# Causal layer of a four-layer kernel: operand loads of batches 1 to 3 moved to ScalarE's queue in column pieces, scores and maxima alternated, block sums of first tiles put later

## The chip, the cores and the metric

One core of a Trainium2 chip runs the whole program in one launch. The metric is device time in microseconds (us), the median of three runs; lower is better.

## The reference, cut to what matters

x has shape (4, 512, 128): four batches of 512 tokens. Four layers are added to it in turn: a selective-scan layer, an attention layer with a mixture of experts, the **causal layer** that this change touches, and the attention and expert layer once more. The causal layer is:

```
h = layernorm(x);  q, k, v = split(h @ Wqkv.T + bqkv)      # 16 heads of 8
q, k = rotary(q), rotary(k)                                # first 2 of the 8 dims
probs = softmax(q @ k.T / sqrt(8) + causal_mask)
L = eye - strict_lower(probs);  rhs = diag(probs) * v
A = solve_triangular(L, rhs, lower=True)
x = x + concat_heads(A) @ Wd.T + bd
```

So row i of A depends on all rows before it: the layer is a forward substitution over the 512 positions of each batch, with the softmax's normalisation carried beside it.

## The kernel before, in words

The causal layer is `delta_phase`. A batch has four tiles of 128 positions (`TPB` = 4), 16 tiles in all, numbered n = 0 to 15, with t = n % 4 the place of the tile in its batch. All engines run one loop over n from -6 to 15, each turn of it divided into 14 hooks h = 0 to 13. Every engine executes its instructions in the order written, so the hooks are the schedule; there is no planner. Turn n solves tile n: `from_earlier` (h = 0, the part that comes from the batch's earlier tiles), `turn_right_side` (h = 1), `inverse` (h = 2) and seven `hop`s (h = 3, 5, 7, 9, 10, 11, 12), each followed on VectorE by `turned_hop`. At h = 12 ScalarE copies the result (`solved`, L2439) and at the start of the next turn it copies the turned result into `a_all` (`turned`, L2443), which the next tile's `from_earlier` on TensorE (L2880) reads.

Around this chain, `beside` prepares later tiles. For tile m = n + 3 TensorE computes the scores (`score`, L2789 and L2798) and ScalarE their exponentials (L2389, L2394); for tile m = n + 3 (t = 0) or n + 4 it computes the scores once more without shift, for the row maxima (`for_maximum`, L2768 and the mask L2771), which VectorE reduces (L2546). The functions `scores_in` and `maxima_in` say which groups fall to which hook; within a hook TensorE issues all scores, then all maxima. Scores leave through two PSUM banks, maxima through three. VectorE adds up the exponentials of the tile's own block (`block_sums`, L2582), then `own_sum`, `spread_sums`, and from these `inverted_sums`, with which GpSimd inverts 16x16 blocks (`inverse_block`); SyncE carries them through DRAM (`inverses`, L2296 and L2303) into `xT`, which `multiplied` (L2832, h = 9 to 12 of the turn before) reads.

The operands `q_op` and `k_op` hold one batch: for each head, 72 rows of three-part bf16 queries or keys by 512 positions, in one buffer each. In turn n = 4b - 4 (n = 0, 4, 8) SyncE stores the split queries and keys of batch b into `q_scr` and `k_scr` (`store_parts`, L2257), waits for these stores, and then runs `operands(b)`: for each half of the heads, once the last tile's scores of that half are done, one DMA of queries (L2271, 576 KB) and three of keys (L2274, 192 KB each). TensorE waits for a half at the first maximum of tile 4b that uses it (groups 0 and 2, at h = 3 and h = 5 of turn 4b - 3). Behind `operands`, SyncE's next work is `inverses(n + 2)` of the turn that follows. For batch 0 another way is used: three pieces by columns (positions), the queries of the first two on SyncE's queue (L2264), the keys and the last queries on ScalarE's (L2367, L2371).

The block sums of a tile with t = 0 are taken at h = 0 and 1 of turn m - 2; its own sum at h = 1, spread at h = 3, inverted at h = 4.

The functions as they stand before, with the line numbers of the profile:

Of the kernel before, what the change touches and what calls it, by code (L numbers as in the profile page):

```python
# [6 lines left out]

# [1914 lines left out]
def delta_phase(core, nc):  # L1922
# [4 lines left out]
    with ExitStack() as ctx:  # L1927
        def sb(name, shape, dt=F32):
# [48 lines left out]
                 "first_in0 first_in1 first_in2 op_in0 op_in1 bias_out m_split diff_out eii_out vn_out m_stored m_in_even m_in_odd sums_out z_out z_spread e_stored e_in "  # L1977
# [56 lines left out]
        def in_program(n):  # L2034
            return 0 <= n < TILES_N
# [28 lines left out]
        def block_sums_in(n, h):  # L2064

            first, second = n + 2, n + 3
            if second == 0:
                return [(0, 2 * (h - 11)), (0, 2 * (h - 11) + 1)] if h in (11, 12) else []
            if first == 0:
                return [(1, 2 * (h - 8)), (1, 2 * (h - 8) + 1)] if h in (8, 9) else []  # L2070
            if in_program(first) and first % TPB == 0 and h < 2:
                return [(first, 2 * h), (first, 2 * h + 1)]
# [28 lines left out]
        def spread_at(m):  # L2101
            return {0: (-3, 13), 1: (-2, 13)}.get(m, (m - 2, 3))

        def own_sum_at(m):
            return {0: (-3, 13), 1: (-2, 12)}.get(m, (m - 2, 0 if m % TPB else 1))

        def inverted_at(m):
            return {0: (-2, 1), 1: (-1, 1)}.get(m, (m - 2, 4))
# [86 lines left out]
        with nc.Block() as block:  # L2195
# [56 lines left out]
            def _(sp):  # L2252
# [14 lines left out]
                def operands(b):  # L2267
                    for half in range(2):
                        sp.wait_ge(s["act_ps"], in_act("score", b * TPB - 1, DIAG_GROUPS + (half + 1) * NH // 2 - 1))
                        heads = heads_of(half)  # L2270
                        sp.dma_start(q_op[0:QK_ROWS, heads, :], query_rows(q_scr[b, :, :, heads, :])).then_inc(  # L2271
                            s[f"op_in{half}"], 16)
                        for i in range(PARTS):
                            sp.dma_start(k_op[rows_of_part(i), heads, :], key_rows(k_scr[b, :, :, heads, :])).then_inc(  # L2274
                                s[f"op_in{half}"], 16)

# [31 lines left out]
                for n in range(-LEAD, TILES_N):  # L2308
# [8 lines left out]
                    if in_program(n + 4) and n % TPB == 0:  # L2317
                        store_parts((n + 4) // TPB)
                        if n + 4 == 0:
                            first_queries()  # L2320
                        else:
                            operands((n + 4) // TPB)
# [8 lines left out]
            def _(act):  # L2331
# [30 lines left out]
                def first_keys():  # L2362
                    act.wait_ge(s["parts_stored"], 16 * 2 * PARTS)
                    act.wait_ge(s["pad_in"], 32)
                    for piece, cols in enumerate(FIRST_COLS):
# [3 lines left out]
                        if piece == 2:  # L2369
                            for i in range(PARTS):  # L2370
                                act.dma_start(q_op[i:QK_ROWS:PARTS, :, cols], query_columns(q_scr[0, :, :, :, cols])).then_inc(  # L2371
                                    s[f"first_in{piece}"], 16)

# [75 lines left out]
                for n in range(-LEAD, TILES_N):  # L2449
# [6 lines left out]
                    for h in range(HOOKS):  # L2456
# [258 lines left out]
            def _(pe):  # L2715
# [40 lines left out]
                def for_maximum(n, g):  # L2756
# [6 lines left out]
                    if n >= TPB and t == 0 and g * heads in (0, NH // 2):  # L2763
                        pe.wait_ge(s[f"op_in{2 * g * heads // NH}"], 16 * (1 + PARTS) * b)
# [72 lines left out]
                def beside(n, h):  # L2837
# [13 lines left out]
                    for i in scores_in(n, h):  # L2851
                        score(n + 3, i)
                    for m, hd in maxima_in(n, h):
                        for_maximum(m, hd)
# [183 lines left out]
```

## Time and profile before

| | |
|---|---|
| median of 3 runs | 1435.49 us (1435.31 to 1438.86) |
| profiled execution, its own time | 1435.48 us |
| its span, first to last instruction | 1433.6 us |
| TensorE busy | 1141.3 us (80%) |
| VectorE busy | 987.3 us (69%) |
| ScalarE busy | 684.4 us (48%) |
| GpSimd busy | 630.1 us (44%) |
| mean granted TensorE clock | 0.887 of full |
| causal layer | from about 628 to 1108 us of the span |

Times in the rows are microseconds from the start of the span. "Idle before" in brackets is how long the engine stood before that instruction, and what released it. Busy shares say little here: TensorE is busy most of the time, and what a change in the causal layer is worth is read from the places where TensorE stands still.

### The profile page before, as it was taken

To read this page: it belongs to the slowest core of one execution; us is meant where nothing else is said; L and a number is where in the kernel's file an instruction comes from. 1 tells how busy PE (TensorE), PEld (TensorE's weight loads), DVE (VectorE), ACT (ScalarE), POOL (GpSimd) and SP (SyncE) were. 2 spreads that over 40 slices of the span, in tenths; PEclk is the share of its full clock that TensorE was granted. 3 is DMA by queue.
4 is the path that set the end of the run, shared out by engine and by line. 5 is a ranking of instruction groups with operands and counts; after the bars stand their busy time and mean duration, and the time that the engine had idled before them with its cause. 6 is when DMAs were issued, how large, how long until landed. Compare 5 with 4: busy or idle time off the path is not lost. (4 is left out here: it accounts for less than half of the span.)

```text
span 1433.6 us, 32921 instructions
## 1 busy us (share of the span) xinstructions
PE 1141.3 (80%) x12875; PEld 621.9 (43%) x12906; DVE 987.3 (69%) x2114; ACT 684.4 (48%) x1412; POOL 630.1 (44%) x838
## 2 busy tenths in 40 slices
PE   6746767769999998833767988878986799999975
PEld 2212222323333335822555665656665233333375
DVE  5699999978888875544745746646521798888453
ACT  3843334414776776621442442343341277676744
POOL 2268979954235212521632533533441533251153
PEclk9869979978999999865898978989987599999988
DMA  5388934132141402244242141141120232240222
GB/s 154 134 287 317 330 118 179 37 90 57 37 105 55 105 3 91 66 99 89 32 85 46 28 107 26 29 105 26 28 44 11 70 91 58 68 119 22 86 56 87
DMA packets 133279, 128.22 MB, mean 89 GB/s; under 512 B 87543, under 2 KB 119095, under 8 KB 127738
## 3 DMA queue, kind: packets, MB, share of 16 engines
q1 hardware_dynamic: 125072, 118.24, 29.8%
q0 software_dynamic: 2496, 5.13, 1.1%
q10 hardware_dynamic: 5558, 2.76, 0.9%
q8 instruction: 102, 1.67, 0.5%
q14 instruction: 51, 0.42, 0.1%
HBM read 105.42 MB, written 38.49 MB: 100 GB/s over the span
## 5 line engine op out<-in xcount | busy, mean ns | idle before, releaser
L1402 DVE TENSOR_REDUCE f_row_min<-f_ps 128x1 f32<-128x512 f32 x512 | 327.7, 682 | 63.8 <-PE f_ps L1722 63.1
L1284 ACT ACTIVATE f_e<-f_ps 128x512 f32<-128x512 f32 x512 | 278.7, 598 | 124.3 <-PE f_ps L1741 123.4
L1722 PE MATMUL f_ps<-f_operands 72*128 72x512 bf16 x512 | 205.0, 411 | 20.5 <-DMA f_operands<-k_scr 15.3
L1741 PE MATMUL f_ps<-f_operands 75*128 75x512 bf16 x512 | 190.0, 381 | 2.6 <-ACT f_e L1284 2.6
L789 PE MATMUL m_ps<-m_shared,sb_ident 128*128 128x512 f32 x256 | 134.7, 674 | 60.6 <-DVE m_shared L629 60.6
L362 POOL TENSOR_TENSOR m_drive<-m_du,m_ring 128x1024 f32<-128x1024 f32 x64 | 149.5, 2349 | 57.1 <-DVE m_ps L621 37.5
L2546 DVE TENSOR_REDUCE d_row_min<-d_ps 128x1 f32<-128x384 f32 (+3 forms) x176 | 105.2, 635 | 60.6 <-PE d_ps L2771 59.1
L494 ACT ACTIVATE m_ps<-m_delta,m_A 128x511 f32<-128x511 f32 x128 | 83.0, 681 | 132.7 <-DVE m_ps L621 109.0
L1752 PE MATMUL f_ps<-f_e,f_v_op 128*32 128x512 f32 x1024 | 137.2, 607 | 2.4 <-ACT f_e L1284 1.4
L1722 PEld LDWEIGHTS f_ps<-f_operands 72*128 72x128 bf16 x512 | 51.3, 101 | 162.9 <-DVE f_row_min L1402 111.8
L789 PEld LDWEIGHTS m_ps<-m_shared,sb_ident 128*128 128x128 f32 x256 | 52.2, 214 | 145.4 <-DVE m_shared L629 89.5
L621 DVE TENSOR_TENSOR_SCAN m_ps<-m_ps,m_drive 128x1024 f32<-128x1024 f32 x44 | 101.1, 2297 | 4.9
L2768 PE MATMUL d_ps<-d_k_op,d_q_op 96*128 96x128 bf16 (+3 forms) x256 | 68.2, 346 | 29.4 <-DMA d_k_op<-k_scr 17.0
L2696 DVE STREAM_TRANSPOSE d_a_hop<-d_ps 128x32 f32<-128x32 f32 x112 | 23.8, 213 | 83.6 <-PE d_ps L2921 71.5
L2921 PE MATMUL d_ps<-d_mT,d_a_hop 16*32 16x16 f32 (+3 forms) x3584 | 67.6, 209 | 8.4 <-DVE d_a_hop L2696 7.5
L2225 POOL TENSOR_TENSOR d_xT_blk<-d_xT_blk,d_prod 128x14 f32<-128x14 f32 (+6 forms) x224 | 64.7, 289 | 17.6
L1172 POOL DMA_INDIRECT y_scr<-f_operands x46 | 53.5, 1164 | 40.5 <-DVE f_operands L1612 38.5
L1741 PEld LDWEIGHTS f_ps<-f_operands 75*128 75x128 bf16 x512 | 49.6, 99 | 49.1 <-ACT f_e L1284 20.3
L2214 POOL TENSOR_TENSOR d_xT_blk<-d_e_blk,d_zi_blk 128x256 f32<-128x256 f32 x16 | 14.3, 893 | 126.1 <-DVE d_zi_blk L2611 124.0
L2220 POOL TENSOR_TENSOR d_prod<-d_xT_blk 128x14 f32<-128x14 f32 (+6 forms) x224 | 60.6, 271 | 17.6
L2832 PE MATMUL d_ps<-d_xT,d_e_nat 128*32 128x128 f32 (+3 forms) x2048 | 58.6, 263 | 12.1 <-DMA d_xT<-x_scr 5.4
L1146 POOL DMA_INDIRECT f_rows_scr<-f_h2n,f_place_u x32 | 31.7, 990 | 82.6 <-DVE f_place_u L1520 74.9
(297 smaller groups left out, 2162.7 us busy)
## 6 DMA issues: line engine op xcount, KB each, us to landing
m_ring<-bc_scr SPq DMA_DIRECT2D x32, 1024.0 KB, 5.2
f_rows_scr<-blank SPq DMA_DIRECT2D x2, 8707.5 KB, 31.4
f_wall<-f_wall SPq DMA_DIRECT2D x16, 578.0 KB, 5.0
f_operands<-q_scr SPq DMA_DIRECT2D x32, 288.0 KB
f_operands<-k_scr SPq DMA_DIRECT2D x96, 96.0 KB
d_q_op<-q_scr SPq DMA_DIRECT2D x6, 576.0 KB
d_k_op<-k_scr SPq DMA_DIRECT2D x18, 192.0 KB
f_operands<-f_rows_scr SPq DMA_DIRECT2D x46, 64.5 KB, 1.9
```

Source lines behind the costliest of these rows:

```text
L362: nc.gpsimd.tensor_tensor(drive[:, step % AHEAD, :].rearrange("p (a s) -> p a s", a=HALVES), du[:, :, tokens(b)], b_row(step).unsqueeze(1) ...
L494: last = nc.scalar.activation(ps[:, at + 1:at + S], delta[:, k, b * S + 1:(b + 1) * S], ACT.Exp, scale=A[:, k, n:n + 1])
L621: nc.vector.tensor_tensor_scan(h, bank(DECAY + HALVES * (step % 2), HALVES), drive[:, step % AHEAD, :], 0.0, ALU.mult, ALU.add).then_inc(s ...
L789: last = nc.tensor.matmul(bank(Y + k), core.ident[:, :], hC[:, k * S:(k + 1) * S], start=False, stop=last_of_batch)
L1284: nc.scalar.activation(e_sb[:, n % 3, hh, :], ps[:, SCORE[(b * UNITS + u) % SCORE_BANKS], :], ACT.Exp, scale=SCALE).then_inc(s["e_out"], 1)
L1402: nc.vector.tensor_reduce(row_min[:, b % 2, u // TPB, u % TPB:u % TPB + 1], ps[:, MAXQ[(b * UNITS + u) % MAX_BANKS], :], AX.X, ALU.max, ne ...
L1722: nc.tensor.matmul(ps[:, MAXQ[n % MAX_BANKS], :], q_op(b, QK)[:, hd, t * P:(t + 1) * P], k_op(b, QK)[:, hd, :], start=True, stop=True).the ...
L1741: nc.tensor.matmul(ps[:, SCORE[n % SCORE_BANKS], :], k_op(b, QKS)[:, hd, t * P:(t + 1) * P], q_op(b, QKS)[:, hd, :], start=True, stop=True ...
L1752: last = nc.tensor.matmul(ps[hh * HEAD_COLS:(hh + 1) * HEAD_COLS, O_BANK, :], v_of(b, t, g * GROUP + hh), e_sb[:, n % 3, hh, :], start=(t ...
L2546: nc.vector.tensor_reduce(row_min[:, n % 2, g * heads:(g + 1) * heads], dve_bank("maximum", n, g)[:, 0:heads * cols].rearrange("p (h c) -> ...
L2768: nc.tensor.matmul(bank[:, hh * cols:(hh + 1) * cols], q_op[0:SHIFT_AT, hd, rows_of(t)], k_op[0:SHIFT_AT, hd, 0:cols], start=(hh == 0), st ...
L2921: last = nc.tensor.matmul(ps[q * SPAN:(q + 1) * SPAN, STEP[n % 2], r * SPAN + cols.start:r * SPAN + cols.stop], a_hop[own, g * SPAN:(g + 1 ...
```

## The change

For the batches 1, 2 and 3, `operands` is gone from SyncE. ScalarE issues the loads instead, twelve DMAs for each batch in four steps by columns: queries of positions 0 to 383 after h = 12 of turn 4b - 4, keys of positions 0 to 127 after its h = 13, and after h = 1 of turn 4b - 3 the keys of positions 128 to 511 and the queries of 384 to 511. Each step is three DMAs. The first six count on one semaphore, for which the first maximum of tile 4b waits; the last six on another, for which the first maximum of tile 4b + 1 waits (h = 6 of the same turn). In each hook TensorE now takes one score and one maximum in turn. The block sums of tiles with t = 0 (but the first) move from h = 0 and 1 to h = 2 and 3, their own sum from h = 1 to 3, spread from 3 to 4 and inversion from 4 to 5.

```
@@ -4,6 +4,7 @@
 
 
 from contextlib import ExitStack, contextmanager
+from itertools import zip_longest
 
 import numpy as np
 
@@ -1974,7 +1975,7 @@
         aT = sb("aT", [P, 2, P])
 
         names = ("set zero_set pad_in ln_stats ln_mv ln_var ln_rstd ln_done swapped rot1 rot2 rot3 prod_out split_q split_k parts_stored "
-                 "first_in0 first_in1 first_in2 op_in0 op_in1 bias_out m_split diff_out eii_out vn_out m_stored m_in_even m_in_odd sums_out z_out z_spread e_stored e_in "
+                 "first_in0 first_in1 first_in2 first_cols_in other_cols_in bias_out m_split diff_out eii_out vn_out m_stored m_in_even m_in_odd sums_out z_out z_spread e_stored e_in "
                  "blk_step x_stored x_in g_ps gT_sb gn_ps gn_sb at_ps hop_in at_sb an_ps an_sb "
                  "act_ps act_out dve_ps dve_out").split()
         s = {n: core.sem("d_" + n) for n in names}
@@ -2068,8 +2069,8 @@
                 return [(0, 2 * (h - 11)), (0, 2 * (h - 11) + 1)] if h in (11, 12) else []
             if first == 0:
                 return [(1, 2 * (h - 8)), (1, 2 * (h - 8) + 1)] if h in (8, 9) else []
-            if in_program(first) and first % TPB == 0 and h < 2:
-                return [(first, 2 * h), (first, 2 * h + 1)]
+            if in_program(first) and first % TPB == 0 and h in (2, 3):
+                return [(first, 2 * (h - 2)), (first, 2 * (h - 2) + 1)]
             if in_program(second) and second % TPB and h in (8, 9, 12, 13):
                 return [(second, (8, 9, 12, 13).index(h))]
             return []
@@ -2099,13 +2100,13 @@
             return (-2, 12) if m == 1 else (m - 2, 2)
 
         def spread_at(m):
-            return {0: (-3, 13), 1: (-2, 13)}.get(m, (m - 2, 3))
+            return {0: (-3, 13), 1: (-2, 13)}.get(m, (m - 2, 3 if m % TPB else 4))
 
         def own_sum_at(m):
-            return {0: (-3, 13), 1: (-2, 12)}.get(m, (m - 2, 0 if m % TPB else 1))
+            return {0: (-3, 13), 1: (-2, 12)}.get(m, (m - 2, 0 if m % TPB else 3))
 
         def inverted_at(m):
-            return {0: (-2, 1), 1: (-1, 1)}.get(m, (m - 2, 4))
+            return {0: (-2, 1), 1: (-1, 1)}.get(m, (m - 2, 4 if m % TPB else 5))
 
         def batch_at(place, n, h):
             return next((b for b in range(B) if place(b) == (n, h)), None)
@@ -2264,16 +2265,6 @@
                             sp.dma_start(q_op[i:QK_ROWS:PARTS, :, cols], query_columns(q_scr[0, :, :, :, cols])).then_inc(
                                 s[f"first_in{piece}"], 16)
 
-                def operands(b):
-                    for half in range(2):
-                        sp.wait_ge(s["act_ps"], in_act("score", b * TPB - 1, DIAG_GROUPS + (half + 1) * NH // 2 - 1))
-                        heads = heads_of(half)
-                        sp.dma_start(q_op[0:QK_ROWS, heads, :], query_rows(q_scr[b, :, :, heads, :])).then_inc(
-                            s[f"op_in{half}"], 16)
-                        for i in range(PARTS):
-                            sp.dma_start(k_op[rows_of_part(i), heads, :], key_rows(k_scr[b, :, :, heads, :])).then_inc(
-                                s[f"op_in{half}"], 16)
-
                 def shifts(n):
                     t = n % TPB
                     sp.wait_ge(s["act_out"], in_act("shifts", n))
@@ -2318,8 +2309,6 @@
                         store_parts((n + 4) // TPB)
                         if n + 4 == 0:
                             first_queries()
-                        else:
-                            operands((n + 4) // TPB)
                     if in_program(n + 4) and (n + 4) % TPB != 0:
                         shifts(n + 4)
                     if in_program(n + 3) and (n + 3) % TPB == 0:
@@ -2370,6 +2359,17 @@
                             for i in range(PARTS):
                                 act.dma_start(q_op[i:QK_ROWS:PARTS, :, cols], query_columns(q_scr[0, :, :, :, cols])).then_inc(
                                     s[f"first_in{piece}"], 16)
+
+                def queries(b, cols, after, done):
+                    act.wait_ge(s["act_ps"], all_scores(after))
+                    act.wait_ge(s["parts_stored"], 16 * 2 * PARTS * (b + 1))
+                    for i in range(PARTS):
+                        act.dma_start(q_op[i:QK_ROWS:PARTS, :, cols], query_columns(q_scr[b, :, :, :, cols])).then_inc(done, 16)
+
+                def keys(b, cols, after, done):
+                    act.wait_ge(s["act_ps"], all_scores(after))
+                    for i in range(PARTS):
+                        act.dma_start(k_op[rows_of_part(i), :, cols], key_rows(k_scr[b, :, :, :, cols])).then_inc(done, 16)
 
                 def own_exponential(n):
                     act.wait_ge(s["diff_out"], n + 1)
@@ -2459,6 +2459,16 @@
                             from_earlier(n)
                         if n >= 0 and HOP_AFTER.get(h) == HOPS:
                             solved(n)
+                        b = starts_in(n, 4)
+                        if b is not None and b >= 1:
+                            if h == 12:
+                                queries(b, slice(0, S - P), TPB * b - 2, s["first_cols_in"])
+                            if h == 13:
+                                keys(b, slice(0, P), TPB * b - 1, s["first_cols_in"])
+                        b = starts_in(n, 3)
+                        if b is not None and b >= 1 and h == 1:
+                            keys(b, slice(P, S), TPB * b - 1, s["other_cols_in"])
+                            queries(b, slice(S - P, S), TPB * b - 1, s["other_cols_in"])
 
             @block.vector
             def _(dve):
@@ -2760,8 +2770,10 @@
                         pe.wait_ge(s["pad_in"], 32)
                     if n < len(FIRST_COLS) and g == 0:
                         pe.wait_ge(s[f"first_in{n}"], 16 * 2 * PARTS)
-                    if n >= TPB and t == 0 and g * heads in (0, NH // 2):
-                        pe.wait_ge(s[f"op_in{2 * g * heads // NH}"], 16 * (1 + PARTS) * b)
+                    if n >= TPB and t == 0 and g == 0:
+                        pe.wait_ge(s["first_cols_in"], 16 * 2 * PARTS * b)
+                    if n >= TPB and t == 1 and g == 0:
+                        pe.wait_ge(s["other_cols_in"], 16 * 2 * PARTS * b)
                     bank = dve_free("maximum", n, g)
                     for hh in range(heads):
                         hd = g * heads + hh
@@ -2848,10 +2860,11 @@
                     m = maxima_done(n, h - 1)
                     if m is not None:
                         turn_shifts(m)
-                    for i in scores_in(n, h):
-                        score(n + 3, i)
-                    for m, hd in maxima_in(n, h):
-                        for_maximum(m, hd)
+                    for i, maximum in zip_longest(scores_in(n, h), maxima_in(n, h)):
+                        if i is not None:
+                            score(n + 3, i)
+                        if maximum is not None:
+                            for_maximum(*maximum)
                     if in_program(n + 1) and h in MT_HOOKS:
                         multiplied(n + 1, MT_HOOKS.index(h))
                     m = later_tile_at(sums_at, n, h)
```

## Rows read from the trace of the kernel before

**Rows 1.** Turns 1 and 3 by stretch: length, busy (x) of PE, PEld, DVE, ACT, POOL, PEclk, DMA share, GB/s.

```profile
740.40:775.50 35.10, 23.27 (x577) 16.87 (x582) 12.31 (x39) 5.34 (x16) 9.58 (x31) 0.81 0.43 78
...
797.80:824.40 26.60, 24.82 (x614) 17.74 (x616) 17.51 (x42) 11.27 (x25) 13.75 (x41) 0.98 0.17 30
```

**Rows 2.** Waits of PE, 640 to 1110: us in total, times, longest.

```profile
PE d_ps L2768 <- DMA d_k_op<-k_scr: 17.0, 5, 5.1
```

**Rows 3.** Timeline of PE, batch 1: start, us, instructions, idle before.

```profile
744.09 0.37 PE L2880 MATMUL d_ps<-d_e_off,d_a_all 128*32 128x128 f32 x3
...
752.69 0.61 PE L2768 MATMUL d_ps<-d_k_op,d_q_op 96*128 96x128 bf16 x4 [5.13 <-DMA d_k_op<-k_scr]
...
759.69 0.61 PE L2768 MATMUL d_ps<-d_k_op,d_q_op 96*128 96x128 bf16 x4 [4.02 <-DMA d_k_op<-k_scr]
...
762.95 0.60 PE L2768 MATMUL d_ps<-d_k_op,d_q_op 96*128 96x256 bf16 x2
```

**Rows 4.** Timeline of PE, batch 2.

```profile
854.42 1.06 PE L2880 MATMUL d_ps<-d_e_off,d_a_all 128*32 128x128 f32 x32
...
857.66 0.40 PE L2768 MATMUL d_ps<-d_k_op,d_q_op 96*128 96x128 bf16 x4
...
864.67 0.61 PE L2768 MATMUL d_ps<-d_k_op,d_q_op 96*128 96x256 bf16 x2
```

**Rows 5.** Timeline of PE, batch 3.

```profile
956.86 0.82 PE L2880 MATMUL d_ps<-d_e_off,d_a_all 128*32 128x128 f32 x18
...
962.47 0.40 PE L2768 MATMUL d_ps<-d_k_op,d_q_op 96*128 96x128 bf16 x4 [1.18 <-DMA d_k_op<-k_scr]
...
968.95 0.61 PE L2768 MATMUL d_ps<-d_k_op,d_q_op 96*128 96x128 bf16 x4 [4.72 <-DMA d_k_op<-k_scr]
...
972.20 0.60 PE L2768 MATMUL d_ps<-d_k_op,d_q_op 96*128 96x256 bf16 x2
```

**Rows 6.** Timeline of SP's queue: first operand load of batches 1, 2, 3.

```profile
740.04 0.86 SPq L2271 DMA_DIRECT2D d_q_op<-q_scr  x1
...
845.58 0.88 SPq L2271 DMA_DIRECT2D d_q_op<-q_scr  x1
...
951.91 0.85 SPq L2271 DMA_DIRECT2D d_q_op<-q_scr  x1
```

**Rows 7.** Timeline of ACT at the end of turns 0, 4, 8.

```profile
741.06 0.27 ACT L2443 COPY d_a_all<-d_ps 128x128 f32<-128x128 f32 x1 [0.42 <-PE d_ps L2931]
...
850.97 0.27 ACT L2439 COPY d_aT<-d_ps 128x128 f32<-128x128 f32 x1
...
953.40 0.27 ACT L2439 COPY d_aT<-d_ps 128x128 f32<-128x128 f32 x1
```

**Rows 8.** Timeline of ACT's DMA issues for batch 0.

```profile
651.19 7.59 ACTq L2367 DMA_DIRECT2D d_k_op<-k_scr  x9
...
658.81 4.31 ACTq L2371 DMA_DIRECT2D d_q_op<-q_scr  x3
```

**Rows 9.** Stretches with operand loads (columns as in rows 1): batches 1, 2, 0.

```profile
740.00:760.00 20.00, 9.69 (x245) 7.31 (x239) 2.97 (x11) 1.44 (x5) 3.86 (x13) 0.79 0.66 127
845.00:861.00 16.00, 13.03 (x403) 10.86 (x395) 4.37 (x14) 3.17 (x9) 3.69 (x10) 0.82 0.66 160
...
652.00:668.40 16.40, 7.69 (x39) 4.62 (x39) 7.66 (x17) 0.47 (x2) 1.94 (x2) 0.57 0.87 144
```

**Rows 10.** DMA packets, 740 to 760, then 652 to 668.5.

```profile
DMA packets 531, 2.54 MB, mean 127 GB/s; under 512 B 112, under 2 KB 240, under 8 KB 240
...
DMA packets 7156, 2.37 MB, mean 144 GB/s; under 512 B 4883, under 2 KB 7155, under 8 KB 7155
```

**Rows 11.** Timeline of DVE, turn 2.

```profile
779.90 1.27 DVE L2582 TENSOR_REDUCE d_z_col<-d_e_nat 128x4 f32<-128x512 f32 x2
```

**Rows 12.** Waits of PE, turn 6.

```profile
PE d_ps L2832 <- DMA d_xT<-x_scr: 1.6, 1, 1.6
PE d_ps L2908 <- DVE d_g_pad L2687: 1.3, 1, 1.3
```

More of the change, by code:

```diff
@@ L6 @@
 from contextlib import ExitStack, contextmanager
+from itertools import zip_longest
 import numpy as np
@@ L2070, in block_sums_in @@
                 return [(1, 2 * (h - 8)), (1, 2 * (h - 8) + 1)] if h in (8, 9) else []
-            if in_program(first) and first % TPB == 0 and h < 2:
-                return [(first, 2 * h), (first, 2 * h + 1)]
+            if in_program(first) and first % TPB == 0 and h in (2, 3):
+                return [(first, 2 * (h - 2)), (first, 2 * (h - 2) + 1)]
             if in_program(second) and second % TPB and h in (8, 9, 12, 13):
@@ L2265, in first_queries @@
                                 s[f"first_in{piece}"], 16)
[L2267 to L2275, printed above, removed]
                 def shifts(n):
@@ L2320, in _ @@
                             first_queries()
-                        else:
-                            operands((n + 4) // TPB)
                     if in_program(n + 4) and (n + 4) % TPB != 0:
@@ L2372, in first_keys, with queries, keys @@
                                     s[f"first_in{piece}"], 16)
+                def queries(b, cols, after, done):
+                    act.wait_ge(s["act_ps"], all_scores(after))
+                    act.wait_ge(s["parts_stored"], 16 * 2 * PARTS * (b + 1))
+                    for i in range(PARTS):
+                        act.dma_start(q_op[i:QK_ROWS:PARTS, :, cols], query_columns(q_scr[b, :, :, :, cols])).then_inc(done, 16)
+                def keys(b, cols, after, done):
+                    act.wait_ge(s["act_ps"], all_scores(after))
+                    for i in range(PARTS):
+                        act.dma_start(k_op[rows_of_part(i), :, cols], key_rows(k_scr[b, :, :, :, cols])).then_inc(done, 16)
                 def own_exponential(n):
@@ L2461, in _ @@
                             solved(n)
+                        b = starts_in(n, 4)
+                        if b is not None and b >= 1:
+                            if h == 12:
+                                queries(b, slice(0, S - P), TPB * b - 2, s["first_cols_in"])
+                            if h == 13:
+                                keys(b, slice(0, P), TPB * b - 1, s["first_cols_in"])
+                        b = starts_in(n, 3)
+                        if b is not None and b >= 1 and h == 1:
+                            keys(b, slice(P, S), TPB * b - 1, s["other_cols_in"])
+                            queries(b, slice(S - P, S), TPB * b - 1, s["other_cols_in"])
             @block.vector
@@ L2850, in beside @@
                         turn_shifts(m)
[L2851 to L2854, printed above, removed]
+                    for i, maximum in zip_longest(scores_in(n, h), maxima_in(n, h)):
+                        if i is not None:
+                            score(n + 3, i)
+                        if maximum is not None:
+                            for_maximum(*maximum)
                     if in_program(n + 1) and h in MT_HOOKS:
```

14 lines of the change are left out of this document (8 added, 6 removed).

## The prediction

> **What bounds the kernel now.** I read the page first, for the share of each engine, and then went to the causal layer alone, since only that is touched. TensorE executes in order and carries the chain of the substitution, so a turn lasts as long as TensorE needs, its standstills included. The stretches by turn show this: turn 3, with scores and maxima side by side, has TensorE busy 24.8 of 26.6 us, while turn 1, the first after an operand load, takes 35.1 us with 23.3 busy [rows 1]. The reader is to see that the time to be had is in the turns 1, 5 and 9, not in turn 3. TensorE's waits over the whole layer name the cause: 17.0 us in five waits for the keys [rows 2].
>
> The timelines of these turns show what the waits hang on. In batch 1 TensorE stands 5.1 us before the first maximum of tile 4 (free from 747.56) and 4.0 us before the third group, and reaches the first maximum of tile 5 at 762.95 [rows 3]. In batch 2 the first maximum comes without a wait at 857.66, the tile after at 864.67 [rows 4]. In batch 3 the waits are 1.2 and 4.7, the first maximum of the next tile is at 972.20 [rows 5]. That leaves 17.0 - 5.1 - 4.0 - 1.2 - 4.7 = 2.0 us for batch 2's second half; the work after that wait is the same as from 759.69 to 762.95, 3.3 us, so that half was in by 864.67 - 3.26 = 861.4. The queue of SyncE began the loads at 740.04, 845.58 and 951.91 [rows 6]. From first issue to the last operand the loads thus take 19.7, 15.8 and 17.0 us, mean 17.5. The second half is the one that decides, and tile 4b + 1 starts 3.3 us after it has landed.
>
> **The operand loads.** The same bytes move (2304 KB), so the question is when they start, how long they last and who must wait for the last of them.
>
> Start. ScalarE issues the first six DMAs after its copy `solved` of h = 12. This copy ends at 741.06 - 0.42 = 740.64 in batch 1, and at 851.24 and 953.67 in batches 2 and 3 [rows 7]. Against SyncE's starts [rows 6] the loads begin 0.6, 5.7 and 1.8 us later. The wait for the parts' stores costs ScalarE nothing, since SyncE had passed the same wait before those moments; behind it stand `turned` and `from_earlier`, which the chain needs.
>
> Issue. Nine of ScalarE's issues for batch 0 took 7.59 us, 0.84 each; the last three, queued behind all the others, 4.31, that is 1.44 each [rows 8]. These are the bounds: 5.0 to 8.6 us for six. With an emptier queue I take the lower, 5.0. They lie in front of `turned`, so `a_all` comes at 745.9 instead of 741.3. TensorE's `from_earlier` started only at 744.09 because other sums came first [rows 3], so the chain moves by 745.98 - 744.09 = 1.9 us, not by 5. In the same way by 2.2 in batch 2 (854.42, [rows 4]) and 2.1 in batch 3 (956.86, [rows 5]). TensorE is then ready for tile 4b at 749.5, 859.9 and 963.4 (962.47 - 1.18 + 2.1). The last six issues follow the copy for h = 0, end by about 753, and ScalarE's next needed work (h = 7) comes later; they cost nothing unless an issue costs 1.44.
>
> Duration. Batch 0 is loaded by columns already, in two thirds of its DMAs by runs of 256 bytes. It moved 144 GB/s against 127 and 160 in the loads by heads [rows 9], with 7156 packets against 531 [rows 10]; from 651.19 to 668.4 it took 17.2 us. In the new form a quarter of the bytes go in 256-byte runs, in batch 0 half; I take 0.7 us off: 16.5. New beside the load is `inverses`, no longer queued behind it: 128 KB for `xT` (L2303) now move at the same time, 128/2304 of 17.5 us = 1.0 us. Sum 17.5 us from the end of `solved` to the last operand; from below 13.5 (the first 1.2 us and 2.36 MB at 200 GB/s, above any whole load of rows 9), from above 20.7 (the 19.7 of batch 1 and the 1.0).
>
> At this place a rule speaks against the change. The Trainium skill, page "DMA: Bandwidth & Descriptors", section Specifications, wants at least 512 bytes in a transfer for line rate, and its section "Rules for kernel authors" says that spreading DMAs over SP and ACT brings no bandwidth, for they end on the same 16 engines. On the first the trace doesn't agree at this size: 144 GB/s in small runs beside 127 in large ones. On the second no stretch contradicts it, and my sum gives the queue no bandwidth. By the first the duration would be at the upper end, which is a rival below.
>
> Who waits. Tile 4b needs the first half (queries to 383 and keys to 127, 1.18 MB), which by half the duration is in at about 750, 860.7 and 963.4: hardly later than TensorE is ready. TensorE then works 6.2 us to tile 5 in batch 1 (3.0 from 752.69 to the second wait, 3.3 behind it), about 5.1 in the others: ready at 755.9, 865.8 and 968.5. The rest lands at 740.64 + 17.5 = 758.1, at 868.7 and at 971.2, later in all three, so the new wait, at the first maximum of tile 4b + 1, ends last. Against 762.95, 864.67 and 972.20: -4.8, +4.0 and -1.0, sum **-1.8 us**. The gain is that 3.3 us of work now lie before the last landing and not behind it; in batch 2 the later start eats it. Bounds by the durations: -9.7 (data in by 754.1, 864.7 and 967.2, TensorE ready later; deltas -7.1, +1.1, -3.7) and +7.8 (three times 3.2, less 1.8).
>
> **The clock.** In the stretch of batch 1's load the granted clock was 0.79 and in turn 1 0.81, while turn 3 had 0.98 [rows 1, 9]: it falls between the waits. The new waits are shorter in batch 1 (2.2 us instead of 9.1) and of 2.9 and 2.7 us in the others. I take **-1.0 us**; bounds 0 and -4.
>
> **Scores and maxima in turn.** The order changes only where a hook has several scores: turns -1, 3, 7 and 11. In turns 2, 6, 10 a hook has one score, and in turns 0, 1, 4, 5 scores and maxima do not meet. In turn 3 TensorE is idle 26.60 - 24.82 = 1.8 us in all [rows 1]; that is the upper bound, and a reordering that starves the exponentials could cost as much. I take -0.2 for each of four, **-0.8 us**, bounds -3 and +2.
>
> **Block sums later.** In turn 2 VectorE does two pairs of block sums, 1.27 us each [rows 11], before it adds the right side; in turn 6 TensorE waits 1.3 us for that sum [rows 12]. The edit removes this wait, but puts the 1.27 us in front of `turned_hop` of h = 2 and h = 3, where VectorE is nearly full. In turn 6 TensorE also waits 1.6 us for `xT` [rows 12], which hangs on SyncE's order and would take back what is gained before it. I take **0**; bounds for three batches -3.9 and +3.9. Spread and inversion one hook later delay GpSimd's block inversion by about 2 us, which is hidden: its result is wanted a turn later.
>
> **Sum.** -1.8 - 1.0 - 0.8 + 0 = -3.6. Against the profiled execution's own 1435.48 us (span 1433.6 and 1.9 around it; the median of the runs, 1435.49, is the same) that is 1431.9, so **1432 us**.
>
> **Rivals.** (1) The load is quicker by columns. If its rate is 200 GB/s, the new waits vanish, -9.7 us; with a clock that stays up (-3) and the order of scores (-0.8) the time is 1422. For it: one load by heads reached 160 GB/s with few rows in flight, and the runs are now longer than batch 0's. Against it: no load of the trace came near. (2) The load is as slow as batch 1's or the small runs hurt: 20.7 us from `solved`, +7.8 instead of -1.8, no help from the clock, 1435.5 + 7.8 - 0.8 = 1442. This is also what the page's rule on 512 bytes would do. For it the 127 GB/s of batch 1, against it the 144 of batch 0 [rows 9]. (3) The other side by ScalarE: its issues cost 1.44 us each. Twelve take 17.3 us, 1.9 lie between the sixth and the seventh, and the last needs some 2 us to land: 21.2 us from `solved`, 3.7 more than forecast in each batch, +11.1 - 1.8 - 0.8 = +8.5, **1444**. It decides as soon as an issue costs over (17.5 - 3.9)/12 = 1.13 us, because then the issue and not the transfer ends last. For it the last three of batch 0, against it the nine before [rows 8].
>
> **Chances.** Forecast 0.40, rival 1 0.30, rival 2 0.16, rival 3 0.14. The likeliest case alone spans 1427 to 1438. What a measurement here can tell from no change is about 0.3%, 4.3 us: below 1431.2 faster, above 1439.8 slower. Of the forecast's 0.40, 0.12 lie below, 0.26 within, 0.02 above; rival 1 is all faster; rivals 2 and 3 give 0.25 slower and 0.05 within. Faster 0.42, same 0.31, slower 0.27. The range takes in both sides, 1420 to 1444.
>
> **What would show it.** Right: the waits for keys at tiles 4, 8, 12 gone or under 1 us, a new wait at the first maximum of tiles 5, 9 and 13, longest in batch 2; six ScalarE issues of about 0.84 us between `solved` and `turned`; `from_earlier` some 2 us later; turn 5 longer than 28 us, turn 1 shorter than 35.1; turn 3 within 1 us of 26.6. Wrong: issues above 1.1 us, or a load that ends under 15 or over 19 us after `solved`. A VectorE transpose at h = 3 of turn 2 that makes TensorE wait over 1 us would show the block sums' price.

## The result and the profile after

The changed kernel takes 1443.09 us in the median of 20 runs (1436.07 to 1448.37); the kernel before, run beside it, 1434.3 (20 runs). The ratio is 1.0053, 95% interval 1.0034 to 1.0073: **0.5% slower, some 7.6 us**. Forecast was 1432.0, a small gain. The time lies inside the predicted range, near its upper end; the sign is wrong.

The profiled execution has a span of 1444.6 us (1433.6 before), a mean granted TensorE clock of 0.876 (0.887) and an own time of 1446.39. A turn below reaches from one copy `solved` to the next. The turns are added up by their place in the batch, because the first turn of a batch holds the wait for the operands and the second the later block sums:

| us, sum of turns | 1, 5, 9 | 2, 6, 10 | 3, 7, 11 | 4, 8, 12 | 13 to 15 |
|---|---|---|---|---|---|
| before | 93.8 | 68.9 | 79.3 | 76.9 | 48.1 |
| after | 97.8 | 77.4 | 77.4 | 75.5 | 47.4 |

The turns explain +8.5 of the +11.0 us of span. The rest is -0.6 ahead of turn 1 and +3.1 in the attention layer behind, which the change does not touch. The turns 1, 5 and 9, which hold the loads, cost 4.0 us here, **and the turns 2, 6 and 10, for which the forecast put 0, cost 8.5**.

The turns 1, 2 and 11 of after by stretch (columns as in [rows 1]):

```profile
740.10:773.60 33.50, 26.05 (x585) 18.89 (x585) 12.76 (x39) 5.28 (x15) 9.62 (x31) 0.75 0.46 78
773.60:799.40 25.80, 21.43 (x532) 15.64 (x530) 18.53 (x56) 8.64 (x19) 9.39 (x31) 0.87 0.21 34
...
1018.20:1042.90 24.70, 22.72 (x595) 15.84 (x589) 15.76 (x41) 11.37 (x25) 11.18 (x34) 1.00 0.16 26
```

and the turns 2 and 11 of before:

```profile
775.50:797.80 22.30, 18.81 (x530) 14.09 (x532) 18.15 (x56) 8.73 (x19) 7.80 (x24) 1.00 0.22 33
...
1006.90:1033.40 26.50, 24.10 (x602) 16.82 (x592) 15.92 (x41) 11.30 (x26) 12.09 (x38) 0.96 0.16 27
```

Turn 2 has the same 530 matmuls, but they are busy for 21.4 us instead of 18.8, at a clock of 0.87 instead of 1.00; TensorE stands 4.4 us instead of 3.5. Over the turns 2, 6 and 10 it is busy 64.2 us instead of 56.3 and idle 13.2 instead of 12.6. So nearly all of the 8.5 us is the same work done more slowly. A lost turn has two parts, idle time and slower work behind it, and the waits below show only the first.

TensorE's waits from 640 to 1120 us, after (us in total, times, longest); [rows 2] is their counterpart:

```profile
PE d_ps L2780 <- DMA d_q_op<-q_scr: 15.9, 5, 10.6
PE d_ps L2833 <- DVE d_z_spread L2614: 11.0, 4, 2.8
PE d_ps L2780 <- DMA d_k_op<-k_scr: 8.8, 3, 4.1
PE d_ps L2893 <- ACT d_a_all L2443: 5.0, 3, 1.8
PE d_ps L2921 <- DVE d_g_pad L2697: 2.3, 6, 0.5
```

Of the first row, all but 4.7 belongs to batch 0, which did not change. The wait for keys is halved (17.0 to 8.8), but three others stand beside it: 4.7 for the last queries, 5.0 for `a_all`, and `z_spread` at 11.0 (8.3 of it in turns 2, 6 and 10), which before was 4.9 in all. The place is in the timeline of TensorE, turn 2:

```profile
784.63 0.61 PE L2833 MATMUL d_ps<-sb_in_block,d_z_spread 128*128 128x16 f32 x2 [2.78 <-DVE d_z_spread L2614]
...
785.46 0.63 PE L2801 MATMUL d_ps<-d_k_op,d_q_op 128*128 128x128 bf16 x4
```

The score matmul of the last line took 0.39 us at 781.02, before the stand, and 0.63 after it. The stretches around it show the clock fall from full speed (2.4 GHz) to half (1.2 GHz) and come back:

```profile
778.00:781.70 3.70, 3.41 (x84) 2.37 (x82) 3.70 (x9) 1.23 (x3) 0.00 (x0) 1.00 0.16 20
784.50:788.00 3.50, 3.37 (x40) 2.52 (x43) 1.72 (x9) 0.60 (x1) 0.27 (x1) 0.50 0.35 33
788.00:792.00 4.00, 4.00 (x71) 2.76 (x64) 2.42 (x7) 1.46 (x3) 3.37 (x10) 0.65 0.31 35
792.00:799.40 7.40, 6.16 (x267) 5.01 (x265) 6.33 (x20) 3.66 (x10) 5.75 (x22) 1.00 0.11 26
```

The wait itself is short and takes the place of others; the 7.5 us behind it run at 0.50 and 0.65. What VectorE did ahead of it:

```profile
778.88 1.27 DVE L2592 TENSOR_REDUCE d_z_col<-d_e_nat 128x4 f32<-128x512 f32 x2
...
780.20 0.98 DVE L2556 TENSOR_REDUCE d_row_min<-d_ps 128x1 f32<-128x384 f32 x2
781.10 1.27 DVE L2592 TENSOR_REDUCE d_z_col<-d_e_nat 128x4 f32<-128x512 f32 x2
782.40 0.18 DVE L2597 TENSOR_TENSOR d_z_col<-d_z_col,d_eii 128x16 f32<-128x16 f32 x1
782.49 0.87 DVE L2488 BATCH_NORM_STATS2 d_stats<-x 128x6 f32<-128x128 f32 x4
...
783.40 0.98 DVE L2556 TENSOR_REDUCE d_row_min<-d_ps 128x1 f32<-128x384 f32 x2
784.29 0.28 DVE L2614 TENSOR_TENSOR d_z_spread<-d_z_col,sb_blocks 128x128 f32<-128x128 f32 x1
```

VectorE has hardly a gap from 778.88 to 784.57 (the lines left out are two transposes of 0.20 us). The spread comes last in that queue, and TensorE's `sums_by_block` (L2833, called with the inversion, h = 5 now instead of 4) waits for it. TensorE has other work, but it stands behind this one in program order.

The loads, in ScalarE's timeline of batch 1 ([rows 7] has the copies of before):

```profile
739.73 0.27 ACT L2439 COPY d_aT<-d_ps 128x128 f32<-128x128 f32 x1
739.79 2.59 ACTq L2367 DMA_DIRECT2D d_q_op<-q_scr  x3
742.42 2.36 ACTq L2372 DMA_DIRECT2D d_k_op<-k_scr  x3
744.83 0.27 ACT L2443 COPY d_a_all<-d_ps 128x128 f32<-128x128 f32 x1 [4.83 <-issue]
...
746.30 3.46 ACTq L2372 DMA_DIRECT2D d_k_op<-k_scr  x3
749.85 5.03 ACTq L2367 DMA_DIRECT2D d_q_op<-q_scr  x3
```

and where TensorE meets them, batches 1, 2 and 3 (two waits each; before: [rows 3 to 5]):

```profile
752.53 0.61 PE L2780 MATMUL d_ps<-d_k_op,d_q_op 96*128 96x128 bf16 x4 [4.05 <-DMA d_k_op<-k_scr]
759.01 0.61 PE L2780 MATMUL d_ps<-d_k_op,d_q_op 96*128 96x256 bf16 x2 [0.37 <-DMA d_q_op<-q_scr]
863.11 0.61 PE L2780 MATMUL d_ps<-d_k_op,d_q_op 96*128 96x128 bf16 x4 [2.01 <-DMA d_k_op<-k_scr]
870.46 0.39 PE L2780 MATMUL d_ps<-d_k_op,d_q_op 96*128 96x256 bf16 x2 [1.23 <-DMA d_q_op<-q_scr]
970.05 0.61 PE L2780 MATMUL d_ps<-d_k_op,d_q_op 96*128 96x128 bf16 x4 [2.70 <-DMA d_k_op<-k_scr]
978.79 0.61 PE L2780 MATMUL d_ps<-d_k_op,d_q_op 96*128 96x256 bf16 x2 [3.06 <-DMA d_q_op<-q_scr]
```

### The profile page after: what moved, and what is told of

The parts are those of the page before. It is cut to its first block and busy times, and to the rows that moved or that the text cites. A ratio compares the mean times of both kernels' runs of the same rounds, so it can differ in the third digit from the quotient of the medians.

```text
span 1444.6 us, 32970 instructions
## 1 busy us (share of the span) xinstructions
PE 1159.1 (80%) x12906; PEld 632.5 (44%) x12906; DVE 988.9 (68%) x2114; ACT 685.3 (47%) x1412; POOL 630.2 (44%) x838
## 5 line engine op out<-in xcount | busy, mean ns | idle before, releaser
L2780 PE MATMUL d_ps<-d_k_op,d_q_op 96*128 96x128 bf16 (+3 forms) x256 | 75.8, 371 | 25.0 <-DMA d_q_op<-q_scr 15.9
L2934 PE MATMUL d_ps<-d_mT,d_a_hop 16*32 16x16 f32 (+3 forms) x3584 | 70.6, 214 | 11.8 <-DVE d_a_hop L2706 6.9
L2226 POOL TENSOR_TENSOR d_xT_blk<-d_xT_blk,d_prod 128x14 f32<-128x14 f32 (+6 forms) x224 | 64.7, 289 | 17.5
L2221 POOL TENSOR_TENSOR d_prod<-d_xT_blk 128x14 f32<-128x14 f32 (+6 forms) x224 | 60.8, 272 | 17.6
L2389 ACT ACTIVATE d_e_nat<-d_ps 128x512 f32<-128x512 f32 x64 | 37.3, 597 | 62.9 <-PE d_ps L2801 61.9
```

The source lines that it names most:

```text
L2780: nc.tensor.matmul(bank[:, hh * cols:(hh + 1) * cols], q_op[0:SHIFT_AT, hd, rows_of(t)], k_op[0:SHIFT_AT, hd, 0:cols], start=(hh == 0), st ...
L2934: last = nc.tensor.matmul(ps[q * SPAN:(q + 1) * SPAN, STEP[n % 2], r * SPAN + cols.start:r * SPAN + cols.stop], a_hop[own, g * SPAN:(g + 1 ...
```

## The experiments

Each ratio is against the kernel before, run beside it in five rounds. Turn sums come from one profile each; for 1, 5, 9 they scatter (85.5 to 99.6 in four kernels with identical loads: before, e2, e3 and e11), so there the ratios decide.

| | ratio, 95% interval | 1, 5, 9 | 2, 6, 10 | 3, 7, 11 |
|---|---|---|---|---|
| after | 1.0053, 1.0034 to 1.0073 | 97.8 | 77.4 | 77.4 |
| e1 | 1.0017, 0.9993 to 1.0042 | 100.2 | 67.0 | 78.0 |
| e2 | 1.0041, 1.0017 to 1.0065 | 85.5 | 75.2 | 79.2 |
| e3 | 0.9981, 0.9956 to 1.0006 | 99.6 | 71.4 | 76.0 |
| e4 | 1.0044, 1.0017 to 1.0071 | 97.1 | 68.9 | 79.6 |
| e5 | 0.9968, 0.9938 to 0.9999 | 92.4 | 67.4 | 80.0 |
| e6 | 1.0035, 1.0005 to 1.0066 | 97.6 | 72.9 | 75.2 |
| e7 | **0.9960, 0.9933 to 0.9986** | 88.9 | 68.1 | 77.1 |
| e8 | 1.0041, 1.0011 to 1.0071 | 100.6 | 67.0 | 80.4 |
| e9 | 1.0002, 0.9974 to 1.0030 | 90.5 | 68.3 | 80.4 |
| e10 | 1.0036, 1.0009 to 1.0064 | 94.0 | 67.8 | 79.6 |
| e11 | 1.0025, 0.9998 to 1.0053 | 86.2 | 69.3 | 81.0 |
| e12 | 1.0018, 0.9996 to 1.0041 | 90.8 | 77.4 | 77.0 |

**e1, all but the block sums.** The four places of tiles with t = 0 back in the changed kernel (the pair h in (2, 3) again h < 2, own sum 1, spread 3, inversion 4).

```
-            if in_program(first) and first % TPB == 0 and h in (2, 3):
+            if in_program(first) and first % TPB == 0 and h < 2:
...
-            return {0: (-3, 13), 1: (-2, 13)}.get(m, (m - 2, 3 if m % TPB else 4))
+            return {0: (-3, 13), 1: (-2, 13)}.get(m, (m - 2, 3))
...
```

> The changed kernel with only the block sums back at their old hooks (loads on ScalarE and the alternation stay). Theory A: turns 2, 6, 10 fall from 77.4 to about 69, the ratio to before is 0.999 to 1.003. Theory B: turns 2, 6, 10 stay above 74, ratio 1.004 or more.

The turns 2, 6 and 10 fell from 77.4 to 67.0: their length hangs on the block sums. What is left of the change (loads and order) could not be told from no change.

**e2, the block sums alone** in the kernel before: the mirror image of e1.

> The kernel before with only the block sums of tiles 4, 8 and 12 put two hooks later (own sum at h = 3, spread at 4, inversion at 5). Theory A (the block sums' place is the main loss: in turn 2 TensorE waits at sums_by_block for the spread): turns 2, 6, 10 together 6 to 9 us longer than before's 68.9, a wait of TensorE for L2604 of 2 to 3 us in each, other turns unchanged; ratio about 1.005. Theory B (the loss comes from the loads, and the long turn 2 is their echo: tile 4's scores finish late): turns 2, 6, 10 within 1.5 us of 68.9, ratio 1.000.

1439.7 against 1433.82 us, +5.9, turns 2, 6 and 10 at 75.2, with clocks of 0.93, 0.87 and 0.93. The two waits they trade, 700 to 1120 us:

```profile
PE d_ps L2821 <- DVE d_z_spread L2604: 8.3, 3, 2.8
...
PE d_ps L2908 <- DVE d_g_pad L2687: 2.3, 6, 0.5
```

and the same two in the kernel before, over the same stretch:

```profile
PE d_ps L2908 <- DVE d_g_pad L2687: 6.1, 9, 1.3
...
PE d_ps L2821 <- DVE d_z_spread L2604: 2.2, 3, 0.7
```

**e3, the order alone** in the kernel before.

```
-                    for i in scores_in(n, h):
-                        score(n + 3, i)
-                    for m, hd in maxima_in(n, h):
-                        for_maximum(m, hd)
+                    for i, maximum in zip_longest(scores_in(n, h), maxima_in(n, h)):
...
```

> The kernel before with only scores and maxima issued in turn. Theory A (my term): turns 3, 7, 11 together 0 to 2.5 us shorter than 79.3, nothing elsewhere; ratio 0.998 to 1.000. Theory B (the order starves an engine): the same turns longer, ratio above 1.001.

1430.26 against 1433.82; the interval holds 1. The turns 3, 7 and 11 speak more clearly: 76.8 in the mean of six kernels with the new order, 79.9 in that of eight with the old.

**e4, the loads alone**, on ScalarE's queue as in the change.

> The kernel before with only the operand loads of batches 1 to 3 moved to ScalarE's queue in four column steps. Theory A: turns 1, 5, 9 together about 4 us longer than before's 93.8 (a_all some 5 us after solved, the new wait at tiles 5, 9, 13), turns 2, 6, 10 as before; ratio 1.002 to 1.004. Theory B (loads are the whole loss): turns 2, 6, 10 grow too, ratio 1.005 or more.

1437.73, ratio 1.0044: the loads cost 6.3 us. The waits, 700 to 1120 us:

```profile
PE d_ps L2780 <- DMA d_k_op<-k_scr: 8.4, 3, 3.8
...
PE d_ps L2780 <- DMA d_q_op<-q_scr: 5.7, 3, 3.0
...
PE d_ps L2892 <- ACT d_a_all L2443: 4.8, 3, 1.6
```

By their ratios the parts are worth +5.9 (e2), -2.7 (e3) and +6.3 us (e4), 9.5 in all, against 7.6 for the three together: they add up within the intervals.

**e5, the same column pieces issued by SyncE**, at its old place in the program; each step waits only for the scores that read what it overwrites.

```
+                def operands(b):
+                    sp.wait_ge(s["act_ps"], all_scores(b * TPB - 2))
+                    ...  # three DMAs: queries 0 to 383
+                    sp.wait_ge(s["act_ps"], all_scores(b * TPB - 1))
+                    ...  # keys 0 to 127, keys 128 to 511, queries 384 to 511
```

> The kernel before with the column steps of the change, but issued by SyncE at the old place: queries of 0 to 383 as soon as the parts are stored, then (after the last tile's scores) keys of 0 to 127, keys of 128 to 511, queries of 384 to 511. Order of scores and block sums as before. Theory A (the loads lose by ScalarE: late start and a_all behind six issues): no wait of TensorE for a_all (4.8 us with ScalarE's queue), turns 1, 5, 9 at most before's level, ratio 0.996 to 1.000. Theory B (the column shape itself is slower to land, or all of it collides with the transfers behind it): turns 1, 5, 9 as with the loads on ScalarE, about 98, ratio 1.003 to 1.005.

1428.34 against 1434.54, ratio 0.9968. The same twelve DMAs, behind the same two semaphores, don't lose here what they lose on ScalarE, and the interval is just clear of no change. So pieces by columns are not what costs. The first issue goes out 0.8 us ahead of the copy `solved` in batch 1, 0.2 behind its start in batch 2 and 4.9 ahead in batch 3, where TensorE doesn't wait for the load at all. Two differences were left: ScalarE's issues stand ahead of `a_all`, and they start later.

**e8, late start on SyncE**: e5 with one more wait ahead of the first DMA, for `solved` of turn 4b - 4.

```
+                    sp.wait_ge(s["at_sb"], b * TPB - 3)
```

> As the column steps on SyncE, but SyncE first waits until tile 4b - 4 is solved, so that the loads start where ScalarE would start them, without a single issue on ScalarE. Theory A1 (the late start is the loss): as slow as the loads on ScalarE, ratio 1.003 to 1.005. Theory A2 (the six issues in front of a_all are the loss): near the column steps on SyncE without the wait, within 0.1%. Theory B: no difference to either.

**e10, no issue ahead of `a_all`**: e4 with the first three DMAs after `turned` and the next three after `from_earlier`'s copy.

```
...
                     if later:
                         turned(n - 1)
+                    b = starts_in(n, 3)
+                    if b is not None and b >= 1:
+                        queries(b, slice(0, S - P), TPB * b - 2, s["first_cols_in"])
...
```

> The kernel before with all loads on ScalarE, but none in front of a_all: queries of 0 to 383 right after the copy to a_all, keys of 0 to 127 after the copy for h = 0, the rest after h = 1. Theory A1 (late start): no wait for a_all any more (4.8 us in three waits before), but the time stays, ratio 1.003 to 1.007. Theory A2 (the six issues in front of a_all): ratio back to 0.999 to 1.002.

e8 costs 1.0041, e10 1.0036. In both, nothing stands ahead of `a_all`, and both are as slow as e4. e10's waits, 700 to 1120 us:

```profile
PE d_ps L2779 <- DMA d_k_op<-k_scr: 17.6, 3, 6.7
...
PE d_ps L2779 <- DMA d_q_op<-q_scr: 2.9, 3, 1.4
```

The 4.8 us of `a_all` are gone and the keys take 17.6 instead of 8.4. It is the start that counts, and e8 against e5 shows it: one added wait, and intervals that don't meet. In e8 SyncE's carrying of the inverses is late as well, since it stands behind the loads, but the waits for `xT` are small: 6.3 us from 700 to 1120 against 5.4 before, 1.8 of them in the turns 5 and 9, where before has none. e10 has no such doubt but another: its first three issues come 0.7 us later than e4's, counted from `solved`, and the next three 1.7 to 2.3 later, so it gives up some start for the free `a_all`.

TensorE's busy and idle time in the turns 1, 5 and 9, and the mean of their clocks, show in what form the price is paid:

| loads | kernels | busy | idle | clock |
|---|---|---|---|---|
| by heads, SyncE | before, e2, e3, e11 | 68.3 | 22.9 | 0.85 |
| by columns, ScalarE | after, e1, e4, e6 | 75.0 | 23.2 | 0.76 |
| by columns, SyncE | e5, e7, e12 | 71.6 | 19.1 | 0.80 |
| the same, late | e8 | 76.7 | 23.9 | 0.73 |
| ScalarE after `turned` | e10 | 66.0 | 28.0 | 0.86 |

With ScalarE's loads TensorE stands no longer than with those by heads; nearly the whole price of these turns is the same work at a lower clock. The four kernels of the first row are busy 65.5 to 71.6 us, those of the second 73.4 to 76.3. The early start on SyncE gives back idle time and part of the busy time. e10 keeps the clock and pays by standing. Why the clock is lower with the loads by columns is not shown.

**e9, both queues**: the first six on SyncE as in e5, the last six on ScalarE after h = 1.

> The kernel before with column steps, the first six loads on SyncE at the old place, the last six on ScalarE after h = 1 of the next turn as in the change. Theory A1 (what loses in the change is the late start of the first half): near the column steps all on SyncE, ratio 0.996 to 1.000, no wait of TensorE for a_all. Theory C (ScalarE's pace in the last six, which ends last, is the loss): as the loads on ScalarE, tiles 5, 9, 13 wait 3 us or more, ratio 1.003 or more.

1432.76 against 1435.08, ratio 1.0002 (0.9974 to 1.0030): between the two theories. As theory C had it, TensorE waits for the last queries, 0.9 us at tile 5, 6.0 at tile 9 and 7.3 at tile 13 (735 to 1060):

```profile
PE d_ps L2785 <- DMA d_q_op<-q_scr: 14.2, 3, 7.3
```

ScalarE can issue the last six only after its copy of h = 0, 4.6 to 5.1 us after `solved`, and there the load is late again; the rest of the difference to e5 stays open.

**e6, the inversion one hook later** than in the change (h = 6), which takes `sums_by_block` with it. Does the wait or VectorE's load price the block sums?

```
-            return {0: (-2, 1), 1: (-1, 1)}.get(m, (m - 2, 4 if m % TPB else 5))
+            return {0: (-2, 1), 1: (-1, 1)}.get(m, (m - 2, 4 if m % TPB else 6))
```

> The changed kernel with the inversion of tiles 4, 8, 12 one more hook later (h = 6 instead of 5; block sums at 2 and 3 and spread at 4 stay). Theory A (TensorE loses in the wait at sums_by_block, placed too close behind the spread): the wait for the spread falls from 2.8 us to under 1 in each of turns 2, 6, 10, these together from 77.4 to 70 to 73; ratio to before 1.000 to 1.003. Theory B (VectorE's load in hooks 2 and 3 is the loss, wherever TensorE stands): the wait reappears at a hop (a_hop) or a maximum, turns 2, 6, 10 stay above 75, ratio 1.004 to 1.006.

The wait for `z_spread` is gone, and the turns 2, 6 and 10 take 72.9 instead of 77.4, not 68. Another wait has come in its place:

```profile
PE d_ps L2780 <- DVE d_row_min L2556: 4.6, 4, 1.5
```

VectorE's row maxima are late in h = 2 and 3, and TensorE's next maxima find no free bank. The new waits are half as long, but the clock falls all the same. Turn 6 of e6, its longest stand, and the stretch after it:

```profile
879.25:903.83 24.58, 21.41 (x530) 15.94 (x531) 18.44 (x56) 8.84 (x20) 9.72 (x31) 0.86 0.21 30
...
889.88 0.34 PE L2780 MATMUL d_ps<-d_k_op,d_q_op 96*128 96x384 bf16 x1 [1.45 <-DVE d_row_min L2556]
...
891.80:898.70 6.90, 6.87 (x135) 5.17 (x137) 4.88 (x13) 2.74 (x5) 5.69 (x17) 0.52 0.30 32
```

e6 has back about half of the 8.4 us that later sums cost in these turns (76.7 in the mean of after, e2 and e12, 68.3 in that of the nine kernels that have all four places as before): moving the waiting matmul is not enough. With e11 below, the other half goes with the two pairs of sums in VectorE's hooks 2 and 3.

**e11, the places of own sum, spread and inversion alone**, block sums at h = 0 and 1.

> The kernel before with the block sums of tiles 4, 8, 12 at their old hooks 0 and 1, and only own sum at 3, spread at 4 and inversion at 5. Theory A (the loss in turns 2, 6, 10 needs the two pairs of block sums, 1.27 us each, in hooks 2 and 3): turns 2, 6, 10 at 67 to 70, no wait for the spread over 1 us. Theory B (the later places alone cost): 72 or more.

`z_spread` waits 4.8 us in three, none over 1.6, and the clock holds. Turn 2 of e11:

```profile
772.83:795.64 22.81, 18.37 (x529) 13.70 (x531) 18.31 (x56) 8.62 (x19) 7.85 (x24) 1.00 0.24 39
```

Turns 2, 6 and 10 take 69.3. By the turns, the later places cost little without the later sums; the ratio, 1.0025 with 1 barely inside, does not settle it. In the turns 2, 6 and 10 the clock is 0.86 to 0.93 in all twelve of after, e2, e6 and e12. In the ten kernels with the sums at h = 0 and 1 it is 1.00 in 28 of 30 such turns; the two others, at 0.93, are turn 6 of e3 and of e4, where TensorE stands 3.5 and 1.8 us for `xT`. The length of one stand does not decide by itself: e11 is idle as long as the kernels with later sums (13.9 us in these turns, 14.0 in the mean of after, e2 and e12), with one stand of 1.6 us, and keeps its clock, while e6 loses it behind one of 1.45. What does decide is not shown.

**e12, the whole change with the loads of e5.**

> The change with its twelve loads issued by SyncE at the old place; alternation and later block sums stay. If the parts add: 0.996 (columns on SyncE and alternation) and 1.004 (block sums) give 0.999 to 1.002; turns 2, 6, 10 at 75 to 77, turns 1, 5, 9 at 92 or less. If the block sums' place was a loss only because the loads were late: 0.995 to 0.998.

1436.9 against 1435.08, ratio 1.0018 (0.9996 to 1.0041): within the intervals, e7's gain less the price of the block sums (77.4 in turns 2, 6 and 10 again).

**e7, e5 with the new order, block sums at their old place.**

> The kernel before with the alternation of scores and maxima and the column steps on SyncE. If the parts add (alternation 0.9981, columns on SyncE as above): Theory A 0.994 to 0.998, turns 3, 7, 11 at 76 to 78 and turns 1, 5, 9 at most 93. Theory B: 0.999 to 1.003.

1425.01 against 1434.54, ratio 0.9960 (0.9933 to 0.9986): faster than the kernel before, and far from the changed one's 1.0053. Its SyncE queue in batch 1 and the copy `solved` there, and the same in batch 2:

```profile
740.53 2.74 SPq L2272 DMA_DIRECT2D d_q_op<-q_scr  x3
742.25 0.27 ACT L2442 COPY d_aT<-d_ps 128x128 f32<-128x128 f32 x1
743.32 6.85 SPq L2276 DMA_DIRECT2D d_k_op<-k_scr  x6
750.21 4.14 SPq L2278 DMA_DIRECT2D d_q_op<-q_scr  x3
...
840.56 2.47 SPq L2272 DMA_DIRECT2D d_q_op<-q_scr  x3
...
846.15 0.27 ACT L2442 COPY d_aT<-d_ps 128x128 f32<-128x128 f32 x1
```

The first DMA goes out 1.7 and 5.6 us ahead of `solved`, behind which ScalarE's must stand; in batch 3 it is 0.6 us ahead.

## Why the prediction was wrong

Two steps failed, the block sums at 0 and the loads with their clock at -1.8 and -1.0. The loads' miss is the larger one: alone they cost 6.3 us by e4 (2.4 to 10.2), inside their bound of +7.8. Both went wrong in the same way: the forecast counted waits, and the price came as slower work. The time lies between rivals 2 and 3 (1442 and 1444), but that is no hit for either: their loads of 20.7 and 21.2 us did not come (19.1), and part of the loss is the block sums', which neither has.

- **Block sums later, 0 with bounds of 3.9: one step that failed.** Alone they cost 5.9 us (2.4 to 9.3), above the bound, though the interval reaches below it. The gain was seen rightly: the waits for the right side fell from 6.1 to 2.3 us. What took its place was not priced. The forecast looked at `turned_hop` and at GpSimd's inversion ("hidden") and passed over the small matmul between them, `sums_by_block`, which on TensorE waits for VectorE's spread: 2.8 us in each of three turns, and the clock falls to half behind it. The forecast gave this step no clock term at all, and the clock carries most of its price: 7.9 of 8.5 us in these turns are busy time. The sign the prediction named, a late transpose at h = 3, did not come.
- **Loads, start.** Right: the first issue follows `solved` at once. The 5.7 us of batch 2 were in the sum. That the start is what the loads' price hangs on is what e5 and e8 show.
- **Loads, issue.** Right for the first six: 2.59 + 2.36 = 4.95 us against 5.0, and `a_all` makes TensorE wait 1.7 us a batch (forecast 1.9 to 2.2). The last six were put at 0.84 each and took 8.5 us in batch 1, 1.41 each. All twelve average 1.12 us in batch 1, 0.91 in batch 2 and 1.17 in batch 3, around the 1.13 from which rival 3 was to decide. But the last operands are in only 4.1 to 5.3 us after the last issue ends, where that rival had 2, so the issues did not end last; and e8 loses as much without an issue on ScalarE.
- **Loads, duration.** 17.5 us from `solved` to the last operand were forecast. From the copies' ends (740.00, 852.82, 958.82) it took 19.0, 17.6 and 20.0, and in twelve loads of four kernels (after, e1, e4, e6) 19.1 in the mean: 1.6 too short, 4.8 us in three. The rate was 126, 139 and 126 GB/s, in these three stretches:

```profile
740.00:760.00 20.00, 13.21 (x256) 9.79 (x257) 5.43 (x19) 0.92 (x4) 3.95 (x14) 0.75 0.75 126
852.60:870.60 18.00, 12.18 (x253) 9.05 (x254) 5.44 (x19) 1.13 (x5) 3.97 (x14) 0.81 0.80 139
958.60:978.80 20.20, 11.60 (x252) 8.62 (x252) 5.44 (x19) 1.14 (x5) 4.99 (x17) 0.82 0.80 126
```

  Batch 0's 144 GB/s [rows 9] were taken for all; it was less, and why is not shown. The old loads moved 127 and 160 in batches 1 and 2 [rows 9], and 148 in batch 3 of before:

```profile
951.90:969.00 17.10, 9.35 (x274) 7.41 (x267) 4.20 (x13) 1.44 (x5) 3.76 (x13) 0.90 0.63 148
```

  On SyncE ten loads by columns (e5, e7, e8, e12; two more ended behind no wait) took 18.3 us in the mean from the first issue, where the three by heads took 17.5. So loads by columns were not quicker, which speaks against rival 1; whether the small runs slow them, as rival 2 has it, stays open. Two sums of the forecast are off without moving its result: 1.2 us and 2.36 MB at 200 GB/s give 13.0 and not 13.5 for the lower bound, and no row shows the 1.2; and half of 17.5 us behind `solved` is 749.4, 860.0 and 962.4, not 750, 860.7 and 963.4.
- **Who waits.** Half wrong. The first half of the operands was to be in after half the time, 8.8 us, hidden behind TensorE's other work. It took 12.5, 10.3 and 11.2, so TensorE waits at tile 4b as well: 4.1, 2.0 and 2.7 us where under 1 was forecast. The new wait at tile 4b + 1 was to be longest in batch 2; it was in batch 3.
- **Loads, sum: -1.8, the other step that failed.** Tile 4b + 1 starts 19.0, 17.6 and 20.0 us after `solved`, before 22.3, 13.4 and 18.5 [rows 3 to 5, 7]: -3.3, +4.2, +1.4, in all +2.3 where -1.8 was forecast. The ratio of e4 says +6.3. The means of four kernels each are nearer to it: the turns 1, 5 and 9 take 91.3 us with the loads by heads and 98.2 with ScalarE's. Of these 6.9 us, 6.7 are busy time at a clock of 0.76 instead of 0.85 and 0.2 idle time. A sum made of waits could not see them.
- **Order, -0.8.** Right in sign, too small: -2.7 us by e3's ratio, -3.2 in the turns 3, 7 and 11 by the means. TensorE's idle time in turn 3 was taken for the upper bound, but the gain lies in busy time: in turn 11 22.72 busy of 24.70 us against 24.10 of 26.50 before, idle 2.0 against 2.4. Part of it is the clock: it is 1.00 in 16 of 18 such turns with the new order and in 11 of 24 with the old. Part is there at full clock too: turn 3 has 24.1 to 24.2 us busy with the new order and 24.5 to 24.7 with the old. Why is open.
- **Clock, -1.0.** Wrong in sign: the mean went from 0.887 to 0.876, in turn 1 from 0.81 to 0.75 and in turn 2 from 1.00 to 0.87. The forecast expected shorter waits to raise it in the turns 1, 5 and 9; by the means above it fell there from 0.85 to 0.76, and in the turns 2, 6 and 10, which the forecast did not ask about, it was lost where it had been full.

Not settled: what makes the clock fall in either place, the +3.1 us in the layer behind, and e9.

## What to carry to other kernels

When work moves on a full engine, follow every value it makes to the reader that waits for it in program order, the smallest matmul included; the price is that wait and, where it lets the clock fall, the slower work behind it, so look for turns at full clock that have something to lose. Before you move a load to another queue, ask when that queue is free to start it: here the same twelve DMAs lost 0.4% behind a late start and not with an early one. Don't judge a load by the waits alone; compare busy time and clock as well. Bound a reordering by busy time too, and don't take the duration of one profile for the kernel's: here three turns with identical loads scattered by 14 us.

## What the runs showed of the hardware

Six DMA issues held ScalarE for 5 us, and its next copy could not start before (idle 4.83 us "issue"). The last three issues of a load took longer than the first three, on ScalarE (5.03 us against 2.59, batch 1 of after) and on SyncE (4.14 against 2.74, batch 1 of e7). In turn 2 of before TensorE stood 1.29 us for the right side and the clock stayed at 1.00; after, it stood 2.78 us and the stretch 784.5 to 788.0 ran at 0.50. In e11 it stood 1.61 us there and stayed at 1.00; in turn 6 of e6 it stood 1.45 us, and 891.8 to 898.7 ran at 0.52. The loads by columns in some 6500 to 6900 packets ran at 126 to 139 GB/s, and batch 0, with 7156, at 144; those by heads in 531 to 558 packets at 127, 160 and 148.
